# A graph kernel on one Trainium2 core: late transposing transfers issued by ScalarE into eight places, and an earlier first spread

## What is computed

```
x = layernorm(x + L0(x, adj))          # softmax(Q K^T + mask) V
h = x @ W.T + b_W
e = (h @ a1)[:, None] + (h @ a2)[None, :] + b_a
e = where(e > 0, e, 0.2 * e)
attention = softmax(where(adj > 0, e, -9e15), axis=1)
x = layernorm(x + attention @ h)
```

## Time and profile before

| | us |
|---|---|
| median of 3 runs | 250.46 |
| lowest, highest | 249.81, 250.56 |
| the profiled execution | 250.7 |
| its span, first to last instruction | 248.9 |
| outside the span | 1.8 |

### The profile page before, as it was taken

How to read it: one execution, slowest core, us unless ns; L and a number is a source line. 1 busy time by engine, 2 the same in 40 slices (tenths; PEclk the granted TensorE clock), 3 DMA queues, 4 the chain that set the end, 5 groups by cost and what they waited for, 6 DMA issues and landing times.

```text
span 248.9 us, 3917 instructions
## 1 busy us (share of the span) xinstructions
PE 231.7 (93%) x1425; PEld 128.8 (52%) x1425; DVE 186.1 (75%) x286; ACT 153.8 (62%) x180; POOL 62.8 (25%) x104
## 2 busy tenths in 40 slices
PE   5889999999999999999999999999999994999980
PEld 4786756555555455554554555555544341444460
DVE  1359788886998776979677777887667256999943
ACT  3356987989769996430889991803899853312041
POOL 3365578999600000003210000030300000003531
PEclk9999999999999999999999999999999997999997
DMA  6999999999999999999989999995699999543012
GB/s 173 366 383 374 385 386 382 386 386 385 386 387 384 387 386 384 386 387 385 215 256 394 395 395 387 387 387 190 216 299 289 264 318 232 112 89 84 7 38 90
DMA packets 58794, 75.42 MB, mean 303 GB/s; under 512 B 21651, under 2 KB 26004, under 8 KB 58772
## 3 DMA queue, kind: packets, MB, share of 16 engines
q1 hardware_dynamic: 58336, 75.00, 88.6%
q10 hardware_dynamic: 436, 0.13, 0.3%
HBM read 69.36 MB, written 2.10 MB: 287 GB/s over the span
## 4 chain that ended last, share of the span: by engine, by line
PE 65%; DMA 10%; DVE 8%; ACT 7%; issue 4%; POOL 3%; SPq 1%; ACTq 0%; DVEq 0%; POOLq 0%
PE banks L1269 50%; PE banks L1220 8%; DMA x_tr<-a 8%; DVE e_sb L979 6%; ACT a L789 4%; DMA a_sb<-in_adj_dram 3%; PE banks L1286 3%; PE banks L1170 2%; PE banks L1155 1%; DVE y L1006 1%; PE banks L1141 1%; PE banks L1229 0%; ACT xhat_st L751 0%; POOL f_parts L683 0%; ACT acc_t L798 0%
## 5 line engine op out<-in xcount | busy, mean ns | idle before, releaser
L1269 PE MATMUL banks<-e_sb,f_parts 128*128 128x512 f16 (+1 forms) x786 | 184.2, 384 | 5.5 <-DVE e_sb L979 3.8
L979 DVE SCALAR_TENSOR_TENSOR e_sb<-R,cr_word,banks 128x1024 f32<-128x1024 f32 x96 | 118.7, 1275 | 19.4 <-PE banks L1220 16.5
L789 ACT ACTIVATE a<-a_sb,code_bias 128x2048 fp8e4<-128x2048 int32 x64 | 124.6, 1998 | 12.1 <-DMA x_tr<-a 6.9
L1269 PEld LDWEIGHTS banks<-e_sb,f_parts 128*128 128x128 f16 x786 | 73.2, 96 | 93.5 <-DVE e_sb L979 6.1
L693 POOL TENSOR_TENSOR frstd<-frv,minus_half 128x4 f32<-128x4 f32 x8 | 9.0, 1131 | 161.4 <-DVE frv L1015 160.2
L979 DVE SCALAR_TENSOR_TENSOR e_sb<-R,cr_word,x_tr 128x1024 f32<-128x1024 f32 x28 | 35.0, 1304 | 12.6 <-DMA x_tr<-a 12.6
L1220 PEld LDWEIGHTS banks<-ident,a 128*128 128x128 f16 x384 | 25.1, 97 | 8.7 <-ACT a L789 0.5
L1220 PE MATMUL banks<-ident,a 128*128 128x128 f16 x384 | 28.9, 219 | 0.2 <-ACT a L789 0.2
L776 ACT COPY R<-banks 128x512 f32<-128x512 f32 x7 | 4.1, 585 | 30.2 <-PE banks L1170 30.2
L805 ACT ACTIVATE junk<-y 128x128 f32<-128x128 f32 x28 | 8.3, 297 | 20.4 <-DVE y L1006 20.3
L1155 PE MATMUL banks<-m0c_um,x_tr 128*128 128x130 f32 x64 | 10.5, 317 | 0.0
(11 more groups left out here) (116 smaller groups left out, 106.6 us busy)
## 6 DMA issues: line engine op xcount, KB each, us to landing
a_sb<-in_adj_dram SPq DMA_DIRECT2D x128, 512.0 KB, 10.7
x_sb<-in_x_dram SPq DMA_DIRECT2D x8, 256.0 KB, 8.8
out_dram<-out_sb SPq DMA_DIRECT2D x8, 256.0 KB, 2.6
x_tr<-a SPq DMA_TRANSPOSE x14, 3.3
w_nat<-in_L_gnn_W_dram ACTq DMA_DIRECT2D x1, 64.0 KB, 2.7
wv<-in_L_gnn_Wv_dram ACTq DMA_DIRECT2D x1, 64.0 KB, 3.1
acol<-in_L_gnn_a_vec_dram SPq DMA_DIRECT2D x1, 1.0 KB, 3.2
bcol<-in_L_gnn_b_W_dram ACTq DMA_DIRECT2D x1, 0.5 KB, 3.3
```

Source lines behind the costliest of these rows:

```text
L789: nc.scalar.activation(a_words[:, n % 2, k, :, Q * h:Q * (h + 1), :].rearrange("p e r x -> p r e x"), a_parts[:, m % SLOTS, :, :].rearrang ...
L979: nc.vector.scalar_tensor_tensor(out=e_sb[:, k % NE, :], in0=R[:, g % 2, :], scalar=cr_word[:, 0, 2 * t + b:2 * t + b + 1], in1=word_codes ...
L1269: ins = nc.tensor.matmul(dst, f[:, j, :], e_half[:, k % NE, cols, part], start=(opened and n == 0), stop=(j == T - 1 and n == 2))
```

## The change

It has two parts, which share nothing but the release.

**The late transfers.** The places for the transposed codes move from `x_tr` (four) to `x_sb` (eight), which held x and is free by then. `move` is issued by ACT: after `codes(51)`, `codes(53)`, ... `codes(63)` stand the two moves of the pair of units that these codes complete. SP's list keeps only loads and stores. The wait for a free place is now for the unit eight before.

**The start.** PE runs `layer0(1)` and the first `spread` ahead of the two `half_turn`s and `x_turned(2)`; eight `keep_busy` matmuls go. The first half row is copied to `R` by ACT instead of DVE, between `exps(0)` and `codes(1)`. `ps_exp[0]` moves to bank 7, and `exps(0)` no longer waits for `at_half`. The second `spread` stands between the two halves of `half_sums(1, 0)` instead of ahead of both.

```
-    NM = 4
+    NM = 8
-        ps_exp = [... for i, c in ((4, 256), (2, 160))]
+        ps_exp = [... for i, c in ((7, 0), (2, 160))]
+        x_kept = x_sb[:, :, :].rearrange("p (i q) d -> p i (q d)", q=Q)
+        at_moved = [x_kept[:, i, :].bitcast(F16).rearrange("p (r n) -> p r n", r=TG) for i in range(NM)]
+        code_moved = [x_kept[:, i, :].bitcast(F8).rearrange("p (n b) -> p n b", b=2) for i in range(NM)]
-        at_moved = [x_tr[:, i, :].bitcast(F16).rearrange("p (r n) -> p r n", r=TG) for i in range(NM)]
-        code_moved = [x_tr[:, i, :].bitcast(F8).rearrange("p (n b) -> p n b", b=2) for i in range(NM)]
...
@@ SP @@
-                    if m % 2 == 1:
-                        for u in (m - SLOTS - 1, m - SLOTS):
-                            if by_dma(u):
-                                move(u)
-                for u in range(S - SLOTS, S):
-                    move(u)
...
@@ ACT @@
-                        if i == 0:
-                            act.wait_ge(at_half, 1)
+                def move(s):
+                    n, c = divmod(s, 4)
+                    d = moved(s)
+                    act.wait_ge(codes_ready, PARTS * n + 2 * (c // 2) + 2)
+                    if d >= NM:
+                        act.wait_ge(p_ready, 2 * (s - NM + 1))
+                    else:
+                        act.wait_ge(y0_ready, QUADS)
+                    nc.scalar.dma_start_transpose(out=at_moved[d % NM], in_=a16[:, n % 2, c // 2, c % 2, :]).then_inc(
+                        at_landed[d % NM], 16)
                 exps(0)
+                rows(0, 0, ps_row)
                 codes(1)
...
                         codes(slot + CODES_AHEAD)
+                        if slot % 2 == 1 and by_dma(slot + CODES_AHEAD):
+                            move(slot + CODES_AHEAD - 1)
+                            move(slot + CODES_AHEAD)
@@ DVE @@
-                dve.wait_ge(row_ready, 1)
-                nc.vector.tensor_copy(R[:, 0, 0:HW], ps_row[:, :]).then_inc(r_ready, 1)
@@ PE @@
                 x_turned(1)
+                layer0(1)
+                spread(0, 0, ps_row)
                 half_turn(0, 0)
                 half_turn(1, 0)
-                layer0(1)
                 x_turned(2)
-                keep_busy(ps_row, 8)
-                spread(0, 0, ps_row)
                 pe.wait_ge(xhat_ready, 1)
                 keep_busy(bank[1], 10)
-                half_sums(0, 0)
+                half_sums(0, 0, (0, 1))
                 x_turned(3)
                 half_turn(0, 1)
+                half_sums(1, 0, (0,))
                 spread(0, 1, ps_row2)
-                half_sums(1, 0)
+                half_sums(1, 0, (1,))
                 half_turn(1, 1)
```

More of the change, by code:

```diff
@@ L110, in graph_layers @@
         ps_row2 = bank[6]
-        ps_exp = [bank[i][:, c:c + 2 * Q].rearrange("p (k q) -> p k q", k=2) for i, c in ((4, 256), (2, 160))]
+        ps_exp = [bank[i][:, c:c + 2 * Q].rearrange("p (k q) -> p k q", k=2) for i, c in ((7, 0), (2, 160))]
         ps_last = ps_row[:, 0:2 * P]
@@ L555, in store @@
                     sp.dma_start(out_t[:, 2 * g + q, :, :, :], out_pairs[:, q, :, :, :]).then_inc(stored[q], 16)
[L557 to L567, removed]
                 load_x(0)
@@ L1033, in _ @@
                 half_edges(1, 1, 0)
-                divide(1, inner)
                 for s in range(2):
+                    if s == 0:
+                        divide(1, inner)
                     half_edges(s, 0, 1)
@@ L1230, in half_turn, with half_sums @@
                     ins.then_inc(at_half if h == 0 else at_ready, 1)
-                def half_sums(s, h):
-                    if h == 0:
+                def half_sums(s, h, tiles):
+                    if h == 0 and tiles[0] == 0:
                         if s == 0:
@@ L1238, in half_sums @@
                             pe.wait_ge(parts_ready, 2)
-                    for b in range(2):
+                    for b in tiles:
                         pe.wait_ge(p_half if h == 0 else p_ready, 2 * s + b + 1)
@@ L1329, in _ @@
                 x_turned(1)
+                layer0(1)
+                spread(0, 0, ps_row)
                 half_turn(0, 0)
                 half_turn(1, 0)
-                layer0(1)
                 x_turned(2)
-                keep_busy(ps_row, 8)
-                spread(0, 0, ps_row)
                 pe.wait_ge(xhat_ready, 1)
                 keep_busy(bank[1], 10)
-                half_sums(0, 0)
+                half_sums(0, 0, (0, 1))
                 x_turned(3)
                 half_turn(0, 1)
+                half_sums(1, 0, (0,))
                 spread(0, 1, ps_row2)
-                half_sums(1, 0)
+                half_sums(1, 0, (1,))
                 half_turn(1, 1)
                 layer0(2)
-                half_sums(0, 1)
+                half_sums(0, 1, (0, 1))
                 layer0(3)
@@ L1348, in _ @@
                 turn(2)
-                half_sums(1, 1)
+                half_sums(1, 1, (0, 1))
                 layer0(4)
```

## The result

| kernel | median of the runs | range | profiled execution, span |
|---|---|---|---|
| before | 250.51 us (4 runs) | 249.81 to 251.24 | 250.7, span 248.9 |
| changed | 257.62 us (4 runs) | 257.00 to 257.81 | 257.8, span 256.0 |

The ratio is 1.0279, with an interval from 1.0245 to 1.0314: the change makes the kernel 7 us slower. The forecast was a gain, to 248.1 us (range 245.6 to 252.2). The time went the other way and lies outside the range; it is near the first rival at its full price (256.4).

What follows compares the result with a forecast made beforehand. PE bounds the middle to 178.95 us, then codes, transfers and DVE up to the last edge; profiled 250.7 - 0.85 (start) - 1.5 (end stage) = 248.35, median 248.1 us; 246.2 to 249.6 at 56%, 8-in-10 range 245.6 to 252.2.

Steps and rivals of the forecast that it cites:

- the first rival: Moves of units 50 to 55: ACT's issues as slow as SP's beside loads, up to 9.3 us, 256.4 us; chance 20%.
- the charge for loads beside the issues: First three pairs on ACT, issued while SP issues loads: 0.33 us each, 1.0 us taken off the end stage's gain.
- the near end: Low bound of that charge: a plain issue on ACT at 2.14 us cost 0.78 instead of 0.45, +0.33.
- The far end: High bound of that charge: SP's own first three pairs, 17.3 us where three free pairs are 8.0, +9.3.
- the mark: End of DVE's last edge, 234.51 us before the change; last sums, projection, norm and store hang on it.
- The start: Reordered start of the kernel: second row copy on ACT at 20.9 instead of 21.76, gain 0.85 us, bounds 0 and 1.4.
- The late moves without loads: End stage: ACT becomes the bound at 6.7 us a pair; last edge at 232.0 instead of 234.51, 2.5 us sooner.
- PE's stop and the clock: PE's 3.19 us stop before unit 54 and the lower clock after it: claimed to go.
- Its point of decision: First rival's charge from which it decides: 3.35 us, when the six issues average 1.9 us instead of 1.33.
- The second: Rival: PE's clock falls in the tail, last sums pay 1.5 us or more, 249.6 to 250.3 us; chance 12%.
- The third: Rival: nothing on ACT costs more than SP's best, another 2.4 us off, 245.2 to 245.7 us; chance 12%.
- The fourth: Rival: the start does nothing because the second half row waits for something else, 249.0 us; 8 of the forecast's 56%.

Runs made afterwards that it cites:

- experiment 6: Changed kernel plus three extra 512 KB reads issued by SP together with the moves of units 60 and 61; 260.18 us (one run) against 257.62.
- experiment 1: Kernel before with only the change's new start, late moves still on SP into four places; 249.51 us against 250.76, ratio 0.9958.
- experiment 10: Changed kernel with six moved units instead of fourteen, issued by SP into eight places, new start; 247.09 us, ratio 0.9852.
- experiment 3: Changed kernel with the moves back on SP's queue at their old places in its list, but into eight places; 249.64 us, ratio 0.9956.
- experiment 4: Changed kernel without loads 58 to 63 (last group's column blocks rotated, output not the reference's); 248.76 us (one run).
- experiment 5: Changed kernel with loads 58 to 63 issued as ever but fetching 4 columns instead of 512 (output not the reference's); 249.39 us (one run) against 250.35.
- experiment 8: Changed kernel with eight moved units instead of fourteen, issued by SP into eight places; 245.86 us, ratio 0.9812.
- experiment 9: Changed kernel with ten moved units instead of fourteen, issued by SP into eight places, new start; 245.26 us, ratio 0.9786.
- experiment 7: Changed kernel with eight moved units instead of fourteen, still issued by ACT; 245.84 us, ratio 0.9809.
- experiment 2: Kernel before with only the late moves changed (issued by ACT into eight places), old start; 257.94 us, ratio 1.0289.

## Why the prediction was wrong, by its own steps

**The step that failed is the charge for loads beside the issues.** The prediction bounded it from 1.0 us (the +0.33 of the earlier trace rows for each of three pairs) to 9.3 us (SP's own three pairs, 17.3 against 8.0), and took the near end. Measured it is 17.6 - 8.0 = 9.6 us, on the engine that was the bound. The reason it gave was that in the earlier trace rows the slow issues stood behind loads in the same queue, and ACT's queue holds none. The changed kernel and experiment 6 refute that: the issue is slow although ACT's queue holds no load. The far end was the same operation beside the same loads, in another queue; the near end was another kind of transfer. I chose by the queue and should have chosen by the operation.

The miss on the mark, in sums. The prediction put the last edge at 232.15 (234.51 - 0.85 - 1.5); it is at 241.52, 9.4 us later. Of these 9.6 - 1.0 = 8.6 are that charge. The start gave 0.7 more than predicted. The codes of 63 ended at 231.98 instead of 223.95, 8.0 us late, which is about these two. The other 1.4 us is DVE's. The prediction let it start on unit 60 when the squares were done and counted 4.9 us for 60 and 61; in the rows above it first does residuals (0.60 us, L1003), and 60 and 61 take 5.65, since one edge of unit 60 took 2.06 us where the median of its line is 1.28. The first two edges after the residuals took as long in the kernel before (3.26 us). The last pair took 3.82 us to issue instead of 2.64, but DVE was at units 60 and 61 all that time and then waited 0.21 us for unit 62.

**The start.** Predicted 0.85 us with bounds 0 and 1.4; measured 1.57 at the first full sums, those of unit 4, and 1.25 in the medians of experiment 1. These sums stand in the chain of the changed kernel at 38.78 us, where the earlier trace rows has 40.35 and the prediction 39.5:

```profile
38.78 2.88 PE banks L1265 x12
```

and PE, with the ACT copy that counts, to the earlier trace rows:

```profile
14.06 1.11 PE L1166 MATMUL banks<-ident,cr_word 128*128 128x128 f32 x4 [0.32 <-DVE cr_word L957]
...
15.82 0.63 PE L1137 MATMUL banks<-ident,x_sb 128*128 128x128 f32 x4
16.29 0.72 PE L1317 MATMUL banks<-ident 128*128 128x128 f16 x10
16.84 1.52 PE L1265 MATMUL banks<-e_sb,f_parts 128*128 128x512 f16 x6
...
20.17 0.59 ACT L757 COPY R<-banks 128x512 f32<-128x512 f32 x1 [1.45 <-PE banks L1166]
```

The row copy is at 20.17, not at 20.9. The order of work and the spread at 14.1 were as predicted. Missed was PE's pace: the prediction had the third quad's transpose (L1137) at 0.85 us, its price in the kernel before, and here it takes 0.47 from its start to the next. But the new order doesn't bring that with it. The ten traces that have the new start put unit 4's first sums at 38.78 to 39.47 us, 0.9 to 1.6 before the 40.35. Where this transpose was fast (the changed kernel, experiments 1 and 10) they are at 38.78 to 38.98. Where it ran at the pace of before, 1.06 us (experiments 3, 4, 5, 6, 8 and 9), they are at 39.24 to 39.47; experiment 7 lies between. Experiment 3's rows:

```profile
15.82 1.06 PE L1140 MATMUL banks<-ident,x_sb 128*128 128x128 f32 x4
...
17.47 1.52 PE L1268 MATMUL banks<-e_sb,f_parts 128*128 128x512 f16 x6
```

So the predicted 0.85 is close for six of the ten, and the rest of the 1.57 is when PE's pace rises in the one execution that was profiled. The prediction takes that pace for the clock; the profile's record of the granted clock shows 1.00 from 9 to 18 us in all these traces, so that the clock was the lower one there is read from the matmuls' lengths alone.

**The late moves without loads.** Right, but visible only when the loads are gone: the 6.7 us cycle (6.73 measured), ACT as the bound, SP's price for an issue on a free queue on ACT too (2.64 a pair against 2.67), and the variances waiting for ACT's squares. Not right is the gain of this part with no charge, 2.5 us. In experiment 4 the last edge is 2.2 us before the mark, and in its trace unit 4's first sums are at 39.24, so the start has 1.1 of these; moving the issues thus gains 1.1 us where nothing holds them. What is missing is DVE's own work on units 60 and 61, as above.

**PE's stop and the clock.** Predicted to go; it moved to unit 52 and grew from 3.19 to 4.95 us. The prediction's check had unit 54 with a margin, which it was right to make and which the charge ate: the third pair, issued at about 195 in the prediction, was issued at 199.94 and stood until 205.6.

**The rivals.** The first came true, with its place (units 50 to 55) and its price. It should have had the larger chance. Its point of decision, 3.35 us, was passed nearly threefold. The second (the clock in the tail) didn't decide: in experiment 4 all slices but the very last show the high clock although PE works at half its pace from 222 us on. The third (nothing costs more than SP's best) fell with the first. The fourth (the start does nothing) fell by experiment 1.

**The other queue.** No transfer got faster by going to ACT's queue: the landing takes 3.1 us at least and 4.6 in the median, against 3.0 and 3.3 in the earlier trace rows. The Trainium skill ("DMA: Bandwidth & Descriptors", section "Issuing engines are not separate DMA queues") says that issuing from more engines saves the sequencer's time alone. With that these rows agree. And the changed kernel shows that the sequencer's time saved on SP, up to 5.65 us for a transpose beside loads, is then taken from the new engine.

## What to carry to other kernels

An issue is an instruction of its engine and can stand for microseconds while other queues' transfers are under way; before moving it to an engine with compute behind it, read the longest issues of the same operation in the trace, at their full length, whatever queue they stood in. Put it where nothing that is late stands behind it, or at a time without traffic: the same fourteen moves on SP cost 249.6 us and on ACT 257.6. And when an engine is held up by doing more of a thing by transfers, try fewer: ten instead of fourteen, both on SP with the new start, gained 4.4 us (249.64 to 245.26), where moving the issues of fourteen lost 8.0. Last, a gain at the start of a kernel is read from several traces: here one and the same start gave 0.9 to 1.6 us.

## What was unexpected of the hardware

- A transposing issue (from SBUF to SBUF) took 1.25 us alone and up to 5.65 us beside loads of SP's queue. In the changed kernel it is the second of a pair: cut by small windows, the pairs are 1.53 + 2.78, 1.81 + 5.65 and 1.52 + 4.06 us. In experiment 9, on SP's queue behind the loads, the first of the pair took 6.34 of the 9.88. During the 5.65, from 190.3 to 195.9 us, SP's queue (q1) moved 1.02 MB and ACT's (q10) 0.09, and SP issued nothing at all after 190.23. In experiment 4 ACT's queue moved 0.27 MB in the 2.6 us in which a pair was issued. These are the queues' rows for the two windows, first the changed kernel's (packets, MB, share of 16 engines):

```profile
q1 hardware_dynamic: 532, 1.02, 92.7%
q10 hardware_dynamic: 359, 0.09, 17.6%
```

and experiment 4's:

```profile
q10 hardware_dynamic: 1076, 0.27, 53.8%
```

- A store may do it too. In the changed kernel the last pair's second issue took 2.48 us right behind a store of 256 KB that SP issued at 232.92 us. In the five traces with fourteen moves on ACT in which such a store comes 0.9 us after the last pair's start (the changed kernel, experiments 2, 4, 5 and 6), this pair took 2.92 to 4.21 us, against 2.63 to 2.73 for free ones. No run took the store away, so that it is the cause isn't shown.
- Why the first issue of a pair gets through on ACT and the second is held isn't settled. That the first's packets have to drain before the second's descriptors find room would fit the queue rows above, but no run here varied that.
- With the same order of work at the start, PE's pace doubled at about 15.5 to 16 us in three traces and at about 17 us in six, read from the lengths of its matmuls; that is worth some 0.4 us at unit 4. What decides between them isn't shown.
